# Output projection of two scan layers as 64x64 tiles, written into the places of another tensor's PSUM ring

## The reference

```
seq  = gn(x) as (1024 tokens, 192)
proj = seq @ W_proj.T + b_proj         # 192 x_in, 192 delta, 16 B, 16 C
delta = softplus(delta + dt_bias);  A = -exp(A_log)      # A: 192 x 16
for t in tokens:
    h = exp(delta[t] * A) * h + (delta[t] * x_in[t]) x B[t]   # h: 192 x 16
    y[t] = sum over the 16 states of h * C[t]  +  D * x_in[t]
x = x + (y @ W_out.T + b_out)          # the output projection, then the residual
```

## Time and profile before

| | us |
|---|---|
| median of 3 runs | 4435.09 (4430.67 to 4450.03) |
| the profiled execution | 4430.47 |
| its span | 4428.7 |

### The profile page before, as it was taken

One profiled execution on the slowest core, in us unless ns is written; L12 is line 12 of the kernel. 1 busy time (PEld: TensorE's weight loads), 2 busy tenths in 40 slices (PEclk: granted clock), 3 DMA queues, 4 the chain that ended last, 5 costly groups with the idle time before them and its releaser, 6 DMA issues.

```text
span 4428.7 us, 165322 instructions
## 1 busy us (share of the span) xinstructions
PE 3952.5 (89%) x71984; PEld 2430.5 (55%) x71984; DVE 3265.2 (74%) x3492; ACT 2111.4 (48%) x2771; POOL 2474.9 (56%) x877
## 2 busy tenths in 40 slices
PE   4994898998999984899999999999999999999998
PEld 4994566666666652455555555454454454544554
DVE  6655576665766751688888878888878888888786
ACT  2331444434444432555555555555555555555553
POOL 1121211212112110678888888888888888888887
PEclk9997999999999996789999999899999999999999
DMA  9624232423324221443544534535535435445343
GB/s 102 86 40 101 81 102 70 126 70 95 104 67 115 83 68 47 102 97 86 129 91 99 127 79 105 123 77 118 110 77 127 101 88 126 92 100 125 80 96 72
DMA packets 370756, 419.26 MB, mean 95 GB/s; under 512 B 31401, under 2 KB 283949, under 8 KB 370017
## 3 DMA queue, kind: packets, MB, share of 16 engines
q1 hardware_dynamic: 370050, 408.65, 40.8%
HBM read 267.06 MB, written 91.16 MB: 81 GB/s over the span
## 4 chain that ended last, share of the span: by engine, by line
PE 53%; issue 4%; DVE 2%; ACT 1%; SPq 1%; POOL 0%; DMA 0%; DVEq 0%; POOLq 0%; ACTq 0%
PE ssm_u_ps L789 19%; PE ssm_y_ps L802 16%; PE ssm_scratch L819 8%; PE ssm_scratch L853 6%; DVE ssm_h L1089 1%; PE ssm_scratch L829 1%; PE ssm_scratch L844 1%; DVE ssm_b_diag L1113 1%; SPq L723 1%; ACT ssm_o_sb L1004 1%; PE ssm_scratch L838 0%; PE ssm_scratch L809 0%; DVE ssm_stats L1096 0%; POOL ssm_h L1169 0%; DMA ssm_xn<-const_ones 0%
## 5 line engine op out<-in xcount | busy, mean ns | idle before, releaser
L1169 POOL TENSOR_TENSOR ssm_h<-ssm_h,ssm_c_rep 128x2048 f32<-128x2048 f32 x384 | 1741.9, 4539 | 210.4 <-DVE ssm_h L1089 195.3
L1089 DVE TENSOR_TENSOR_SCAN ssm_h<-ssm_decay,ssm_h,ssm_u_ps 128x512 f32<-128x512 f32 x768 | 945.6, 1259 | 270.0 <-PE ssm_u_ps L789 269.7
L789 PEld LDWEIGHTS ssm_u_ps<-ssm_b_diag,ssm_dx_t 32*64 32x64 f32 x49152 | 830.2, 139 | 569.7 <-issue 566.8
L789 PE MATMUL ssm_u_ps<-ssm_b_diag,ssm_dx_t 32*64 32x64 f32 x49152 | 935.7, 227 | 97.5 <-issue 82.9
L927 ACT ACTIVATE ssm_decay<-ssm_delta_rep,ssm_a_neg 128x1024 f32<-128x1024 f32 x768 | 856.6, 1142 | 320.6 <-DVE ssm_h L1089 317.6
L1089 DVE TENSOR_TENSOR_SCAN ssm_h<-ssm_decay,ssm_u_ps 128x512 f32<-128x512 f32 x768 | 888.9, 1198 | 94.2 <-PE ssm_u_ps L789 72.4
L802 PE MATMUL ssm_y_ps<-ssm_h,ssm_state_sum 128*64 128x512 f32 x3072 | 820.4, 657 | 13.3 <-issue 8.4
L1703 ACT ACTIVATE l_probs<-l_work 128x532 f32<-128x532 f32 (+1 forms) x384 | 217.3, 566 | 562.0 <-PE l_work L1557 555.3
L802 PEld LDWEIGHTS ssm_y_ps<-ssm_h,ssm_state_sum 128*64 128x64 f32 x3072 | 199.0, 145 | 292.7 <-issue 257.9
L1872 DVE RECIPROCAL l_den<-l_den 96x1024 f32<-96x1024 f32 x32 | 209.6, 6548 | 197.4 <-ACT l_den L1716 197.4
L1955 POOL TENSOR_TENSOR l_rstd<-l_var_eps,l_minus_half 96x2 f32<-96x2 f32 x16 | 11.1, 693 | 586.0 <-DVE l_var_eps L1792 586.0
(11 more groups left out here) (162 smaller groups left out, 5705.8 us busy)
## 6 DMA issues: line engine op xcount, KB each, us to landing
ssm_c_rep<-ssm_c_by_state SPq DMA_DIRECT2D x256, 512.0 KB, 6.7
ssm_delta_rep<-ssm_delta SPq DMA_DIRECT2D x384, 128.0 KB, 6.1
l_qk_parts<-l_qk SPq DMA_DIRECT2D x48, 768.0 KB, 4.8
ssm_x<-x_after_l SPq DMA_DIRECT2D x32, 768.0 KB, 6.1
ssm_x_res<-x_after_l SPq DMA_DIRECT2D x192, 128.0 KB
l_x<-x SPq DMA_DIRECT2D x64, 192.0 KB, 8.8
x_after_l<-l_x SPq DMA_DIRECT2D x64, 192.0 KB, 4.1
l_x<-x_after_l SPq DMA_DIRECT2D x16, 768.0 KB, 5.5
```

Of the source, the lines that this page charges most:

```text
L789: made = nc.tensor.matmul(u_ps[64 * par:64 * par + 64, w % U_RING, r - 2 * win, at:at + 64], dx_t[rows, n.s, db, k, 64 * g:64 * g + 64], b ...
L1089: nc.vector.tensor_tensor_scan(h[:, s % S_RING, npi, t], decay[:, 2 * (s % 2) + npi, t], u, start, ALU.mult, ALU.add).then_inc(scanned, 1)
L1169: nc.gpsimd.tensor_tensor(view, view, c_rep[:, 2 * q:2 * q + 2, :], ALU.mult).then_inc(c_applied, 1)
```

## The change

- `project_out` computes a third as twelve matmuls of 64 rows (one g) and 64 columns with 256 moving columns: for each db, four tiles (g, e), where e is the half of 512 tokens. The result goes to a place of u's ring: partitions 64e, bank g. Only the blocks of `w_out` on the diagonal are read.
- The thirds are no longer fills of `scratch`. They run after slots 5, 8 and 11 (OUT_SLOTS), take places of the ring in their turn (USES), and wait for the scan of the window that had the place, three uses back; later uses of u wait accordingly, or for `out_taken` where an output third had the place. Before, the waits were for the scratch bank.
- de.0 moves from slot 11 to slot 9.
- ACT's `take_output` reads both banks of the place and writes `o_sb` with 512 tokens in order.
- POOL's `add_residual` moves from steps 2, 4, 5 to 3, 4, 6.
- The residual is loaded and stored as runs of 512 tokens (2 KB).

```diff
...
 OWN = ["x.2", "dx.1", "dx.2"]
+OUT_SLOTS = [5, 8, 11]
+RING_USES = S_WINDOWS + len(OUT_SLOTS)
+USES = [use for w in range(S_WINDOWS) for use in [("u", w)] + [("out", q) for q, slot in enumerate(OUT_SLOTS) if slot + 2 == w]]
 TURN = 9
...
     slots = {
-        1: ["x.2"], 2: ["dx.1"], 3: ["norm"], 5: ["tail.0"], 6: ["dx.2"], 8: ["tail.1"], 9: ["tail.2"], 11: ["de.0"],
-        13: ["bc"], 14: ["bt"], 15: ["x.0"], 17: ["de.1"], 19: ["de.2"], 20: ["dx.0"], 21: ["x.1"],
+        1: ["x.2"], 2: ["dx.1"], 3: ["norm"], 6: ["dx.2"], 9: ["de.0"], 13: ["bc"], 14: ["bt"], 15: ["x.0"], 17: ["de.1"], 19: ["de.2"], 20: ["dx.0"], 21: ["x.1"],
     }
-    keep = lambda f: not first if f in OWN or f.startswith("tail") else not last
+    keep = lambda f: not first if f in OWN else not last
     return {slot: [f for f in names if keep(f)] for slot, names in slots.items()}
...
         rep_loaded = [sem(f"rep_loaded{db}") for db in range(3)]
         filled = sem("filled")
         drained = sem("drained")
+        out_filled, out_taken = sem("out_filled"), sem("out_taken")
         stats_made = sem("stats_made")
         stats_seen = sem("stats_seen")
         moments_made = sem("moments_made")
...
         def fill(n, name):
             per = len(MAIN_FILLS)
-            if n.first and not name.startswith("tail"):
+            if n.first:
                 return Fill(0, 2 * per, FIRST_FILLS.index(name))
-            if name.startswith("tail"):
-                host = after(n)
-                if is_last(n):
-                    offset = len(FIRST_FILLS) - EARLY + n.s * per + len(flat(slots(n)))
-                    return Fill(n.it, 2 * per, offset + int(name[5:]))
-            else:
-                host = n if name in OWN else before(n)
+            host = n if name in OWN else before(n)
             offset = len(FIRST_FILLS) - (0 if host.first else EARLY) + host.s * per
             return Fill(host.it, 2 * per, offset + flat(slots(host)).index(name))
+        def ring(kind, i):
+            return USES.index((kind, i)) % U_RING
+        def await_place(eng, n, kind, i):
+            use = USES.index((kind, i)) - U_RING
+            if use < 0:
+                if not n.first:
+                    eng.wait_ge(scanned, n.count(SCANS, 2 * use + 2))
+            elif USES[use][0] == "u":
+                eng.wait_ge(scanned, n.count(SCANS, 2 * USES[use][1] + 2))
+            elif n.first:
+                eng.wait_ge(scanned, n.count(SCANS, 2 * USES[use - U_RING][1] + 2))
+            else:
+                eng.wait_ge(out_taken, before(n).count(3, USES[use][1] + 1))
         def await_bank(f):
             if not f.static_first:
...
             return t.rearrange("p (a k j) -> p a k j", a=4, k=4, j=32)
-        def res_rows(t, g):
-            return t.rearrange("(q c) h w -> c q (h w)", c=64).rearrange("c q (a g z) -> g c q a z", a=4, g=2)[g]
+        def res_rows(t, e):
+            return t.rearrange("(q c) h w -> c q (h w)", c=64)[:, :, HALF * e:HALF * e + HALF]
         N_CONSTS = 19
...
                     sp.dma_start(x[:, :, :], image(sources, n).rearrange("(c p) h w -> p c (h w)", p=C)).then_inc(x_loaded, 16)
                 def load_residual(n):
-                    for g in range(2):
+                    for e in range(2):
                         for q in range(3):
-                            sp.dma_start(x_res[64 * g:64 * g + 64, q, :].rearrange("p (a z) -> p a z", a=4),
-                                         res_rows(image(sources, n), g)[:, q]).then_inc(res_loaded, 16)
+                            sp.dma_start(x_res[64 * e:64 * e + 64, q, :], res_rows(image(sources, n), e)[:, q]).then_inc(res_loaded, 16)
                 def store(n):
                     sp.wait_ge(res_added, n.count(3, 3))
-                    for g in range(2):
+                    for e in range(2):
                         for q in range(3):
-                            sp.dma_start(res_rows(image(targets, n), g)[:, q],
-                                         x_res[64 * g:64 * g + 64, q, :].rearrange("p (a z) -> p a z", a=4)).then_inc(out_stored, 16)
+                            sp.dma_start(res_rows(image(targets, n), e)[:, q], x_res[64 * e:64 * e + 64, q, :]).then_inc(out_stored, 16)
                 def store_c(n):
                     await_drained(sp, fill(n, "bc"))
...
                     if db == 0 and win == 0:
                         pe.wait_ge(diag_made, n.count(4, npq + 1))
                     if not (n.first and w < U_RING):
-                        pe.wait_ge(scanned, n.count(SCANS, 2 * (w - U_RING) + 2))
+                        await_place(pe, n, "u", w)
                         pe.sem_inc(window_free, 1)
                     for c in range(8):
                         k, g = divmod(c, 2)
...
                             rows = slice(32 * r, 32 * r + 32)
                             for par in range(2):
                                 at = 256 * g + 64 * k
-                                made = nc.tensor.matmul(u_ps[64 * par:64 * par + 64, w % U_RING, r - 2 * win, at:at + 64],
+                                made = nc.tensor.matmul(u_ps[64 * par:64 * par + 64, ring("u", w), r - 2 * win, at:at + 64],
                                                         dx_t[rows, n.s, db, k, 64 * g:64 * g + 64],
                                                         b_diag[rows, npq, c, par, :], start=True, stop=True)
                                 if c == 7:
...
                                                    ident[:, :])
                     last.then_inc(filled, 1)
-                def project_out(n, q):
+                def project_out(host, n, q):
+                    if host is None:
+                        pe.wait_ge(scanned, n.count(SCANS, SCANS))
+                    else:
+                        await_place(pe, host, "out", q)
                     if q == 0:
                         pe.wait_ge(y_kept, n.count(3, 3))
+                    pe.sem_inc(window_free, 1)
                     for db in range(3):
-                        last = nc.tensor.matmul(scratch[:, :], w_out[n.layer][:, db, q, :], y_sb[:, n.s, db, :],
-                                                start=(db == 0), stop=(db == 2))
-                    last.then_inc(filled, 1)
+                        for g in range(2):
+                            for e in range(2):
+                                rows = slice(64 * g, 64 * g + 64)
+                                last = nc.tensor.matmul(u_ps[64 * e:64 * e + 64, ring("out", q), g, 0:256], w_out[n.layer][rows, db, q, rows],
+                                                        y_sb[rows, n.s, db, 256 * e:256 * e + 256], start=(db == 0), stop=(db == 2))
+                    last.then_inc(out_filled, 1)
                 def make(n, name):
...
                         project_bc(n)
                     elif kind == "bt":
                         turn_b(n)
-                    elif kind == "dx":
+                    else:
                         turn_dx(n, int(i))
-                    else:
-                        project_out(n, int(i))
                 def make_slot(n, slot):
                     for name in slots(n).get(slot, ()):
-                        make(before(n) if name.startswith("tail") else n if name in OWN else after(n), name)
+                        make(n if name in OWN else after(n), name)
                 def prologue(n):
                     for name in FIRST_FILLS:
...
                                 sum_states(before(n), w // 2 + S_STEPS - 2)
                         if w != TURN:
                             make_slot(n, w)
+                        if w in OUT_SLOTS and not n.first:
+                            project_out(n, before(n), OUT_SLOTS.index(w))
                 def early(n):
                     part(n, range(TURN))
...
                     sum_states(n, S_STEPS - 2)
                     sum_states(n, S_STEPS - 1)
                     for q in range(3):
-                        make(n, f"tail.{q}")
+                        project_out(None, n, q)
                 pe.wait_ge(consts_loaded, 16 * N_CONSTS)
                 schedule(pe, prologue, early, late, tail)
...
                                          ACT.Copy).then_inc(drained, 1)
                 def take_output(n, q):
-                    f = fill(n, f"tail.{q}")
                     if q == 0 and not n.first:
                         act.wait_ge(res_added, n.count(3, 0))
-                    await_fill(act, f)
-                    nc.scalar.activation(o_sb[:, q, :], scratch[:, :], ACT.Identity, bias=b_out[n.layer][:, q:q + 1]).then_inc(drained, 1)
+                    act.wait_ge(out_filled, n.count(3, q + 1))
+                    nc.scalar.activation(o_sb[:, q, :].rearrange("p (a g z) -> p a g z", a=2, g=2),
+                                         u_ps[:, ring("out", q), :, 0:256].rearrange("p g (a z) -> p a g z", a=2), ACT.Identity,
```

(15 more changed lines are left out.)

## The result

| | before | changed |
|---|---|---|
| median, same chip | 4432.88 us (4422.32 to 4450.03) | 4390.27 us (4383.86 to 4397.89) |
| profiled execution's span | 4428.7 us | 4386.1 us |

What follows compares the result with a forecast made beforehand. PE bounds the first part of each image pass (slots 5 to 15), DVE the second. 31 passes x 4.05 = 126 us plus 6 for the last image, 132 off 4430.5: 4298.5, or 4303 as median; range 4254 to 4348.

Steps and rivals of the forecast that it cites:

- Fill: Output fill on PE: twelve narrow matmuls, four tiles at a time, take 1.42 us instead of 2.77; range 1.39 to 1.64.
- rival of two tiles at a time: Output fill on PE runs only two tiles at once and takes 2.78 us: total 4421; chance 0.07.
- The ring and the walk: Slots 5 to 17 walked with output fills taking u_ps places: window 17 starts 4.05 us earlier, one 0.49 us wait.
- none in the slots of the new fills: Gaps in PE's issue lie at slots 20 to 4, so none falls where the new output fills stand.
- The step that counted PE's instructions: PE fetches 108 more instructions an image, 3%; bounds +0.7 us (one more gap every third image) to -1.0 us.
- "gaps" rival: SP's late, dense transfers delay PE's instruction fetch once more per image, 2.1 us: total 4369; chance 0.08.
- "clock" rival: PE waiting for scans in slots 5 to 12 loses its clock, 3.6 us a drop: total 4525; chance 0.04.
- Nothing that PE or DVE needs is late: POOL's later add_residual delays step 7's apply_c from 74.7 to 77.3, but holds up neither PE nor DVE.
- From there to the next image DVE runs without idle, so the rest moves forward: After window 17 DVE stays busy until the next image, so the whole 4.05 us gain is kept.
- the 126 forecast: Gain in us over 31 hosted image passes of 4.05 us each.
- The residual's runs: Residual transfers go from 512 B to 2 KB runs, off the path, and are counted as no gain.
- Last image: Its three output fills run alone, 4.3 us back to back instead of 10.0, ending 5.7 us earlier.

Runs made afterwards that it cites:

- experiment 1: Loop over image pairs written out, no jump back: in the changed kernel 0.974, in the kernel before 1.0001, each to the kernel before.
- experiment 2: Changed kernel with POOL's last add_residual moved back from step 6 to step 5: 0.9807 to the kernel before.
- experiment 8: Residual in 512 B pieces again: changed kernel 0.9977; with loop written out and last add_residual in step 5, 0.9731; both to the kernel before.
- both repairs: Changed kernel with the loop written out and the last add_residual in step 5, run twice: 0.972 and 0.9698 to the kernel before.

## Why the prediction was off

- **Fill: right.** 1.46 us where 1.42 was taken, in the bounds 1.39 to 1.64; no wait for the bank. The rival of two tiles at a time is refuted: it wanted 2.78, and so did the rule of the Trainium skill (TensorE: Matmul & The Clock Gate, Part 3, The mechanism) in the way in which the prediction applied it.
- **The ring and the walk: right as far as they went.** Wait at slot 12 0.58 (0.49), DVE before window 11 1.52 us (1.7), window 10 0.89 (1.1).
- **Failed: "none in the slots of the new fills".** The step that counted PE's instructions looked for gaps where the trace of before shows idle time. The jump's 3.7 us show no idle time there, because 4.6 us of long matmuls and a wait lay over them. The change shortened that cover to 1.3 us of short instructions and removed the wait. I didn't ask what else tail.1 hid. Price by experiment 1: 61 to 69 us. Here the "gaps" rival was the nearest, and its cause was another: the gap is the loop's, not SP's. The mechanism of the "clock" rival, slow groups in slots 6 to 12, came with it in six of ten passes, behind a gap in issue instead of a wait for a scan.
- **Failed: "Nothing that PE or DVE needs is late" on POOL.** I asked who waits for POOL's results, not what POOL's operations do to DVE's while they run. Price: 28 to 39 us by experiment 2, of which the diagonals themselves show 25.
- **Failed, of the same kind: "From there to the next image DVE runs without idle, so the rest moves forward".** The third window of the earlier trace rows says otherwise: DVE is busy for 5.49 of 9.65 us there. From 1800 us on DVE's waits for u fell from 342.1 to 228.7 us (113 of the 126 forecast), but those for `y_ps` rose from 64.2 to 115.1, and the diagonals by 27. From the last scan to the end it took 25.8 us before and takes 23.7 now. So -113 + 51 + 27 - 2 = -37 of the 43 measured. This tells where DVE stood, not what held it: with the loop written out the waits for `y_ps` are 72.3 in the changed kernel, but 124.9 in the one before, at the same time as with its loop. From one execution of the changed kernel to another these rows differ by 14 to 21 us.

```profile
DVE ssm_h L1111 <- PE ssm_u_ps L801: 228.7, 165, 17.9
...
DVE ssm_y_sb L1140 <- PE ssm_y_ps L814: 115.1, 58, 8.8
...
PE ssm_u_ps L801 <- issue: 111.1, 75, 5.0
```

and before:

```profile
DVE ssm_h L1089 <- PE ssm_u_ps L789: 342.1, 199, 17.9
...
DVE ssm_y_sb L1118 <- PE ssm_y_ps L802: 64.2, 52, 6.6
...
PE ssm_u_ps L789 <- issue: 82.9, 62, 4.7
```

- **The residual's runs: counted at nothing**, and that holds only without the jump. With it they are worth 0.8%, about 36 of the 43 us measured (experiment 8).
- **Last image: right in kind, too large in size.** The three fills now run back to back, in 6.1 us instead of the 10.0 of the earlier trace rows, but not in 4.3: PE had idled before them and the granted clock was 0.67 over them (1.00 before). From the last scan to the end 2.1 us are gained, not 5.7.

```profile
4372.02 6.12 PE L874 MATMUL ssm_u_ps<-ssm_y_sb,ssm_w_out 64*64 64x256 f32 x72 [0.83 <-issue]
```

The forecast's ratio was 0.970, and the two kernels with both repairs stand at 0.972 and 0.9698. That supports the walk, but the closeness is partly luck. In these two, DVE's waits for u fell by 144 and 136 us, more than the 126 forecast, and part of it was lost again: 15 and 14 us in waits for `y_ps`, 21 and 19 in the diagonals. The missing 89 us of the changed kernel are matched by the two repairs together (78 and 88 us), and not by their sum when each is made alone (about 108), because they overlap.

## What to carry to other kernels

Before shortening work, look up what it covers: list the branches and other long items of the queues in the trace (they show no idle time while they are hidden) and compare each with the work queued before and behind it. When work moves on POOL, compare its new interval with DVE's operations on two SBUF inputs, not only with who waits for its result. A kernel that is bound by PE and has short instructions around a loop's jump is worth trying with the loop written out.

## What was unexpected of the hardware

- A taken branch on PE lasted 3.3 to 4.4 us in the kernels with the jump at slot 8 or 9, and up to 6.3 at slot 18, where one not taken lasted 0.08. It can be followed by a second gap of up to 2.66 us, after 9 or 38 matmul records in the two executions shown.
- A gap of 2.3 to 2.9 us in PE's work was followed by the granted clock of 0.50 in six cases and stayed at 1.00 in four.
- A diagonal of 1.2 us lasts up to 4.5 when POOL's operations follow each other closely: it ends 1.1 us after POOL's first or second one.
- Twelve fp32 matmuls of 64x64x256 on four tiles take 1.46 us, 1.90 ns a column, about half of what the same product takes as three of 128x128x512 (2.77).
- Shorter or longer pieces of a transfer off the path changed the time by 0.8% in one kernel and by 0.1 to 0.3% in another with the same work.
